# Summing |w2| on ScalarE and quantising it by expert on GpSimd, with its transposes and w1's passes in the waits of the last chain

## The reference, cut to what matters

```
def _bit_quant(W):
    scale = jnp.clip(jnp.mean(jnp.abs(W), axis=-1, keepdims=True), 1e-05, None)
    w_q = jnp.clip(jnp.round(W / scale), -1.0, 1.0) * scale
    return W + jax.lax.stop_gradient(w_q - W)
...
x = x + tanh(g_xattn) * attention(ctx, layernorm(x), ...)
x = x + tanh(g_ffn) * (silu(h @ sw1.T) @ sw2.T + gate * (silu(h @ ew1[e].T) @ ew2[e].T))
```

## Time and profile before

| | us |
|---|---|
| median of 3 runs | 617.04 (615.22 to 618.39) |
| the profiled execution | 616.48 |
| its span, first to last instruction | 614.4 |

### The profile page before, as it was taken

The page is one execution under the profiler, slowest core; times in us unless marked ns, Lnnn a source line. Parts: engine busy times, 40 slices in busy tenths (PEclk is TensorE's granted clock), DMA queues, the critical chain, the costliest instruction groups (busy, mean ns, idle before and its releaser), DMA issues.

```text
span 614.4 us, 20156 instructions
## 1 busy us (share of the span) xinstructions
PE 482.3 (79%) x6634; PEld 390.7 (64%) x6635; DVE 496.6 (81%) x1235; ACT 337.3 (55%) x943; POOL 385.8 (63%) x701
## 2 busy tenths in 40 slices
PE   0038999989989989988988998952359798899882
PEld 0015777767767766766776776641129697888882
DVE  6455998898899899899889889859976768777771
ACT  0124555665675775775675675542217566666660
POOL 5004575677887887887788788775203555555554
PEclk9999999999999999999999999995558989999997
DMA  8922122213222222222322321010121212222220
GB/s 225 247 84 81 48 63 82 68 52 90 83 63 79 81 68 71 84 72 65 96 72 62 94 76 39 15 36 19 36 56 44 72 50 66 66 69 69 59 57 13
DMA packets 74078, 44.07 MB, mean 72 GB/s; under 512 B 6866, under 2 KB 71454, under 8 KB 74032
## 3 DMA queue, kind: packets, MB, share of 16 engines
q1 hardware_dynamic: 66240, 32.39, 19.3%
q0 software_dynamic: 4352, 8.53, 4.2%
q10 hardware_dynamic: 3440, 2.55, 1.5%
HBM read 34.32 MB, written 9.65 MB: 72 GB/s over the span
## 4 chain that ended last, share of the span: by engine, by line
DVE 34%; PE 33%; issue 14%; DMA 9%; SPq 5%; POOL 2%; DVEq 1%; ACT 1%; POOLq 0%; ACTq 0%
DVE mx L528 6%; PE PS L1033 6%; DVE sc L533 5%; PE PS L1041 4%; DVE rspread L538 4%; DMA out<-lent,tin 4%; PE PS L1049 4%; PE PS L1023 3%; PE PS L1017 3%; DMA tin<-rows 3%; PE PS L1057 3%; DMA X<-in_x 2%; PE PS L1081 2%; SPq L245 2%; SPq L280 2%
## 5 line engine op out<-in xcount | busy, mean ns | idle before, releaser
L844 ACT ACTIVATE shared<-PS 124x640 f32<-124x640 f32 x128 | 89.4, 698 | 85.7 <-PE PS L1033 85.1
L528 DVE TENSOR_REDUCE mx<-PS 128x8 f32<-128x616 f32 x128 | 101.6, 794 | 17.4 <-PE PS L1023 15.4
L352 POOL TENSOR_TENSOR vm<-lent,ownhead 124x192 f32<-124x192 f32 x128 | 73.1, 591 | 60.9 <-PE PS L1049 59.8
L533 DVE TENSOR_TENSOR sc<-PS,mx 128x616 f32<-128x616 f32 x128 | 102.0, 797 | 3.2
L1033 PE MATMUL PS<-ident,sc 128*124 128x128 f32 x640 | 96.6, 282 | 3.4 <-ACT shared L844 1.5
L450 POOL DMA_INDIRECT out<-lent,tin x72 | 74.0, 1028 | 30.4 <-issue 30.4
L1033 PEld LDWEIGHTS PS<-ident,sc 128*124 128x124 f32 x640 | 70.8, 141 | 19.1 <-issue 16.8
L398 POOL DMA_INDIRECT rows<-pay,pay_i x64 | 68.4, 1068 | 12.1 <-issue 11.4
L538 DVE RECIPROCAL rspread<-PS 128x128 f32<-128x128 f32 x64 | 60.8, 950 | 16.3 <-PE PS L1049 16.3
L1041 PE MATMUL PS<-shared,ownhead 124*32 124x128 f32 x1536 | 55.2, 276 | 16.8 <-DVE X L549 16.7
L364 POOL TENSOR_TENSOR kbd_hi<-kp_hi,rowsel 128x308 fp32r<-128x308 f32 x64 | 45.3, 707 | 22.9 <-DVE kp_lo L521 21.9
(11 more groups left out here) (192 smaller groups left out, 1102.2 us busy)
## 6 DMA issues: line engine op xcount, KB each, us to landing
lent<-in_ctx SPq DMA_DIRECT2D x64, 154.0 KB
tin<-rows SPq DMA_DIRECT2D x72, 66.0 KB, 1.8
X<-in_x SPq DMA_DIRECT2D x8, 512.0 KB, 9.5
ctxq<-in_ctx SPq DMA_DIRECT2D x16, 154.0 KB
lent<-in_ctx SPq DMA_DIRECT2D x16, 128.0 KB
lent<-in_ctx SPq DMA_DIRECT2D x16, 120.0 KB
lent<-in_ctx SPq DMA_DIRECT2D x16, 94.0 KB
lent<-in_ctx SPq DMA_DIRECT2D x16, 86.0 KB
```

The lines of the kernel that those rows point to most:

```text
L352: ins = nc.gpsimd.tensor_tensor(vm[:, j % 2, v], ctxv[:, s, j, 2 * v:2 * v + CH].rearrange("r c (u v d) -> r c u v d", u=2, v=2)[:, :, :, ...
L528: nc.vector.tensor_reduce(mx[:, u], scores_of(u), AX.X, ALU.max).then_inc(mx_done, 1)
L533: nc.vector.tensor_tensor(sc[:, u, 0:2 * GK].rearrange("p (g i k) -> p g i k", g=2, k=SK), scores_of(u), mx[:, u].unsqueeze(3).broadcast_t ...
L844: nc.scalar.activation(PT[:, s, u, :], PS[0:CR, 4:6, :].rearrange("r v c -> r (v c)")[:, 0:CP * P], ACT.Exp, scale=float(1.0 / np.sqrt(HD) ...
```

## The change

|w2| is summed by ACT with nine activations (Abs with a running sum, `sum_w2`) in steps 1 and 2 of quads 1 and 2. DVE makes scales and halves from it in step 1 of quad 3. POOL quantises w2 by expert with three instructions of 128 x 256 each (`quantise_w2`): experts 0 and 1 in steps 0 and 1 of quad 14, 2 and 3 in those of quad 15, and 4 to 8 between the sorts of quad 12 and those of quad 13. The reduction of |w1| moves ahead of the step with image B + 1, its small scalings ahead of place(NQ - 2), and its last pass (the subtraction) behind top_of(NQ - 1). PE transposes w2 in three parts before and among the last chain's matmuls, and ACT copies them. DVE's reduction, four passes and nine copies for w2 are gone.

```diff
@@ gpsimd
+            def quantise_w2(e):
+                pool.wait_ge(w2_halved, 1)
+                ge(pool, w2_step, 2 * e)
+                scale = wabs2[:, e:e + 1]
+                nc.gpsimd.tensor_scalar(plus2[:], w2n[:, e], half2[:, e:e + 1], scale, ALU.is_gt, ALU.mult)
+                nc.gpsimd.tensor_scalar(minus2[:], w2n[:, e], nhalf2[:, e:e + 1], scale, ALU.is_lt, ALU.mult).then_inc(w2_step, 1)
+                pool.wait_ge(w2_step, 2 * e + 1)
+                ins = nc.gpsimd.tensor_tensor(w2n[:, e], plus2[:], minus2[:], ALU.subtract)
+                ins.then_inc(w2_step, 1)
+                if e == NE - 1:
+                    pool.wait_ge(w2_step, 2 * NE)
+                    pool.sem_inc(quantised, 1)
...
                     if j == 3 and nth >= 3:
                         sort(q - 3, 1 - s, 0)
+                    if isinstance(q, int) and q >= NQ - 2 and j < 2:
+                        quantise_w2(2 * (q - (NQ - 2)) + j)
...
             for j in range(1, QB):
                 sort(NQ - 4, 0, j)
+            for e in range(4, NE):
+                quantise_w2(e)
             for j in range(QB):
                 sort(NQ - 3, 1, j)
             root(NQ - 1, 1)
@@ vector
+                if isinstance(q, int) and q == 3 and j == 1:
+                    dve.wait_ge(w2_summed, NE)
+                    dve.wait_ge(tanh_ready, 1)
+                    step(nc.vector.tensor_scalar(wabs2[:], wabs2[:], 1.0 / F, 1e-5, ALU.mult, ALU.max))
...
             step_of(B, 0, False, True, True, 0)
+            dve.wait_ge(ffw_in, 16 * 4)
+            step(nc.vector.tensor_reduce(wabs[:], w1n[:], AX.X, ALU.add, apply_absolute_value=True))
             step_of(B + 1, 1, False, True, True, 0, logits_of=NQ - 2)
             step_of(B + 2, 2, False, False, True, 0, stats_of=NQ - 1)
             choose(NQ - 2)
-            dve.wait_ge(ffw_in, 16 * 4)
-            step(nc.vector.tensor_reduce(wabs[:], w1n[:], AX.X, ALU.add, apply_absolute_value=True))
+            step(nc.vector.tensor_scalar(wabs[:], wabs[:], 1.0 / D, 1e-5, ALU.mult, ALU.max))
...
             place(NQ - 2, 0)
             top_of(NQ - 2)
-            step(nc.vector.tensor_reduce(wabs2[:], w2n[:], AX.X, ALU.add, apply_absolute_value=True))
...
             choose(NQ - 1)
-            nc.vector.tensor_tensor(w1n[:], w1n[:], neg1, ALU.subtract).then_inc(w1_quantised, 1)
             place(NQ - 1, 1)
             top_of(NQ - 1)
+            nc.vector.tensor_tensor(w1n[:], w1n[:], neg1, ALU.subtract).then_inc(w1_quantised, 1)
             step(nc.vector.tensor_tensor(counts[:], base[:], region0[:, 0:E], ALU.subtract))
...
-            step(nc.vector.tensor_tensor(neg2, w2n[:], nhalf2[:].unsqueeze(2).broadcast_to(full), ALU.is_lt))
-            step(nc.vector.tensor_tensor(w2n[:], w2n[:], half2[:].unsqueeze(2).broadcast_to(full), ALU.is_gt))
-            step(nc.vector.tensor_tensor(w2n[:], w2n[:], neg2, ALU.subtract))
-            step(nc.vector.tensor_tensor(w2n[:], w2n[:], wabs2[:].unsqueeze(2).broadcast_to(full), ALU.mult), quantised)
-            for e in range(NE):
-                dve.wait_ge(wT_psum, e + 1)
-                nc.vector.tensor_copy(W2T[:, e], PS[:, 4 + e % 2, 0:F]).then_inc(wT_copied, 1)
@@ scalar
+            def sum_w2(experts):
+                act.wait_ge(ffw_in, 16 * 4)
+                for e in experts:
+                    nc.scalar.activation(work[:, e * F:(e + 1) * F], w2n[:, e], ACT.Abs,
+                                         accum_out=wabs2[:, e:e + 1]).then_inc(w2_summed, 1)
...
+                    if nth in (1, 2) and 0 < j < 3:
+                        sum_w2((0, 1, 2) if (nth, j) == (1, 1) else (3, 4) if (nth, j) == (1, 2) else (5, 6) if j == 1 else (7, 8))
...
+            copy_w2(range(0, 4))
             make_h(NQ - 1, range(QB))
             copy_h(NQ - 1)
+            copy_w2(range(4, 6))
             fill_pay(NQ - 2, 0)
+            copy_w2(range(6, NE))
             exp_logits(NQ - 1)
             fill_pay(NQ - 1, 1)
@@ tensor
             rank_rows(NQ - 2)
+            pe.wait_ge(quantised, 1)
...
+            transpose_w2(range(0, 4))
             transpose_h(NQ - 1, NQ)
+            transpose_w2(range(4, 6))
             pe.wait_ge(placed, NQ - 1)
             logits(NQ - 1)
+            transpose_w2(range(6, NE))
             pe.wait_ge(logits_kept, NQ)
             rank_rows(NQ - 1)
             pe.wait_ge(w1_quantised, 1)
+            pe.wait_ge(wT_copied, NE)
```

More of the change, by code:

```diff
@@ L226, in build @@
         route_step, base_ready, counts_kept, placed = (sem(x) for x in ("route_step", "base_ready", "counts_kept", "placed"))
+        w2_summed, w2_halved, w2_step = (sem(x) for x in ("w2_summed", "w2_halved", "w2_step"))
         w1_quantised, w1T_psum, w1T_copied = (sem(x) for x in ("w1_quantised", "w1T_psum", "w1T_copied"))
@@ L624, in step_of @@
                     top_of(route_of)
+                if isinstance(q, int) and q == 3 and j == 1:
+                    dve.wait_ge(w2_summed, NE)
+                    dve.wait_ge(tanh_ready, 1)
+                    step(nc.vector.tensor_scalar(wabs2[:], wabs2[:], 1.0 / F, 1e-5, ALU.mult, ALU.max))
+                    step(nc.vector.tensor_scalar(half2[:], wabs2[:], 0.5, None, ALU.mult))
+                    step(nc.vector.tensor_scalar(nhalf2[:], wabs2[:], -0.5, None, ALU.mult))
+                    step(nc.vector.tensor_scalar(wabs2[:], wabs2[:], tgf[:], None, ALU.mult), w2_halved)
                 if j == 2 and stats_of is not None:
@@ L652, in _ @@
             choose(NQ - 2)
[L654 to L655 removed]
+            step(nc.vector.tensor_scalar(wabs[:], wabs[:], 1.0 / D, 1e-5, ALU.mult, ALU.max))
+            step(nc.vector.tensor_scalar(half[:], wabs[:], 0.5, None, ALU.mult))
+            step(nc.vector.tensor_scalar(nhalf[:], wabs[:], -0.5, None, ALU.mult))
             place(NQ - 2, 0)
             top_of(NQ - 2)
[L658 to L664 removed]
             full = [P, NE, FB, D]
@@ L927, in _, with copy_w2 @@
             exp_logits(NQ - 2)
+            def copy_w2(experts):
+                for e in experts:
+                    act.wait_ge(wT_psum, e + 1)
+                    nc.scalar.copy(W2T[:, e], PS[:, e % 4, 0:F]).then_inc(wT_copied, 1)
+            copy_w2(range(0, 4))
             make_h(NQ - 1, range(QB))
             copy_h(NQ - 1)
+            copy_w2(range(4, 6))
             fill_pay(NQ - 2, 0)
+            copy_w2(range(6, NE))
             exp_logits(NQ - 1)
@@ L1133, in _, with transpose_w2 @@
             rank_rows(NQ - 2)
+            pe.wait_ge(quantised, 1)
+            def transpose_w2(experts):
+                for e in experts:
+                    if e >= 4:
+                        pe.wait_ge(wT_copied, e - 3)
+                    for f in range(FB):
+                        ins = nc.tensor.transpose(PS[:, e % 4, f * P:(f + 1) * P], w2n[:, e, f * P:(f + 1) * P], ident[:])
+                    ins.then_inc(wT_psum, 1)
+            transpose_w2(range(0, 4))
             transpose_h(NQ - 1, NQ)
+            transpose_w2(range(4, 6))
             pe.wait_ge(placed, NQ - 1)
             logits(NQ - 1)
+            transpose_w2(range(6, NE))
             pe.wait_ge(logits_kept, NQ)
@@ L1146, in _ @@
                 ins.then_inc(w1T_psum, 1)
-            pe.wait_ge(quantised, 1)
-            for e in range(NE):
-                if e >= 2:
-                    pe.wait_ge(wT_copied, e - 1)
-                for f in range(FB):
-                    ins = nc.tensor.transpose(PS[:, 4 + e % 2, f * P:(f + 1) * P], w2n[:, e, f * P:(f + 1) * P], ident[:])
-                ins.then_inc(wT_psum, 1)
             def load_experts(first_tile, n):
```

10 lines of the change are left out of this document (2 added, 8 removed).

## The result

The changed kernel takes 640.32 us in the median of 4 runs (639.34 to 640.68), the kernel before 616.38 (4 runs): 1.0376 times as long, 95% interval 1.0345 to 1.0407. That is slower, as forecast, but by 24 us instead of 10, and above the range. The page of the changed kernel: its span, the busy time of each engine, the chain that ended last by engine, and one group (line, engine, shape, count, busy us, mean ns, idle time ahead of it and its releaser).

A forecast was written before the change was run, and what follows sets the result against it. The tables' end, reached through the root in POOL's queue, was taken to bound the start of the experts' stage. Last chain 7.6, quads 14 and 15 1.7, quads 1 to 3 0.8, less 0.5: 9.6 us on 616.48, 626.0 us; range 618.5 to 633.

The forecast's parts named there:

- SyncE's queue: From tables to first split: pads and tile loads cover DVE's w2 work, so removing it gains only 0.5 us.
- the reserve of 4.9 us: Last chain: PE has the last logits 4.9 us before DVE takes them, so the root's chain may slip that far.
- c: Price of one expert on POOL: 0.57 + 0.57 + 0.72 + 0.1 = 1.95 us, between 1.6 and 3.3.
- the blocking: Last chain: DVE's two large w1 passes hold POOL's sorts ahead of the root of quad 15, 3.1 us.
- The loop: Experts 0 to 3 in quads 14 and 15 make POOL late: +1.7 us, 0.5 to 4 by an expert's price.
- Quads 1 to 3: ACT's sums (0.3 us) and DVE's four small operations (0.5) delay the loop: +0.8 us, 0 to 2.5.
- The w1 reduction: Last chain: moved ahead of the residual, it delays that and every later step of the chain by 2.0 us.
- (b): Rival: POOL's comparisons are dear, an expert costs 2.8 us, time 631 us; chance 0.13.
- (a): Rival: the sorts are not held by DVE's passes, 3.1 us less, time 623.0 us; chance 0.10.
- (d): Rival: POOL lets the root go on time, an expert costing 0.9 us; faster, 615 us; chance 0.06.
- (c): Rival: the reserve takes most of POOL's lateness, expert at 1.5 us, no blocking; no measurable change, 618.9 us; chance 0.09.
- The rule: Skill's inference that DVE's tensor_tensor leaves descriptor generation free, so sorts run at 0.96 us, time 623.0; forecast followed the trace instead.

The follow-up runs named there:

- experiments 1 to 3: changed kernel without the five experts ahead of quad 13's sorts, 628.76 us; without the four in quads 14 and 15, 630.61; without any, 614.41.
- experiment 6: kernel before with only the reduction of |w1| moved ahead of the step with image B + 1: 618.71 us, ratio 1.0042.
- Experiment 1: changed kernel without the five experts that POOL quantises ahead of quad 13's sorts: 628.76 us.
- experiments 10 and 7: kernel before without DVE's four w2 passes, ratio 0.9994; kernel before with ACT summing |w2| and copying transposes, w2's scales made behind the tables, ratio 0.9968.
- experiment 9: changed kernel with the five experts behind the root of quad 15 and w2's transposes and copies behind those of w1: 629.75 us.

## Why the prediction was wrong

**What held.** SyncE's queue, not DVE, sets the time from the tables to the first split: 17.9 us in the changed kernel and 17.9 to 18.0 in experiments 1 to 3, and taking the passes away gave 0.52 us in one profile, 0.1 in another, and nothing that 12 runs can tell. The root behind the experts, in POOL's queue, sets the tables; the reserve of 4.9 us is used up first; behind the last logits the path costs 12.75 us (455.35 to 468.10) where I had 13.1 and before 12.2. The sign, and the place, were right: what failed is the size of two terms.

**The step that failed is the price of an expert on POOL.** I wrote c = 1.95 and bounded it by 3.3; it is 3.44, above even the ceiling: two comparisons of 1.22 (just under the ceiling of 1.24 each), 0.73 for the subtraction (0.72 forecast) and 0.27 of gaps between them where I had 0.1. The nearest row was an affine_select of 0.40 us at 128 columns, and I took 0.57 for 256. It was another instruction with another price, and I had written myself that no tensor_scalar was in the trace. I kept the ceiling of 1.24 a comparison for c but let the range run only from c = 1.5, below my own floor of 1.6, to 3.0.

By the same steps: five experts in the last chain cost 16.9 us instead of 9.75, and 20.65 with the blocking. The blocking was forecast on the sorts, 3.1 us; it fell on the last expert's comparisons, which took 3.33 and 2.85 us beside passes at 433.67 to 439.32 us, 3.7 us in all. Its size was nearly right, by luck: I had drawn it on other instructions, and where POOL meets the passes depends on c.

**The loop.** I had 1.7 us for quads 14 and 15, and 0.5 to 4 as its bounds. The experts cost 8.2 there, twice the upper bound, and c alone does not explain that, for the bound was to hold at c = 3.3. My own steps give more: two experts of 3.2 us, less 1.61 of idle and 1.0 of reserve, are 3.8 us a quad and 7.6 for both. I had counted quad 14 at half a microsecond; it took 5.3. So the second step that failed is the slack I let the loop absorb, above all in quad 14. Quads 1 to 3 cost 2.0 instead of 0.8. ScalarE's sums cost nothing (0.3 forecast): DVE's maxima are 0.56 us late in quad 0, where no sum has run yet, and 0.57 at image 13, behind all of them. At image 14 they are 2.61 late: the four small operations between cost 2.0 instead of 0.5, and that step of 2.0 is in all five profiles of kernels that have them and in none of the other profiles of the table. The remaining 1.8 of the 12.1 us is no part of the change that I can name: 0.55 is there from quad 0 on, and 1.2 gathers between quads 4 and 13, where the other profiles, with the same code there, fall behind that of before by 0.3 to 2.2. The timeline of DVE there in the changed kernel:

```profile
122.69 0.63 DVE L650 TENSOR_SCALAR half<-wabs 128x9 f32<-128x9 f32 x1
123.35 0.63 DVE L651 TENSOR_SCALAR nhalf<-wabs 128x9 f32<-128x9 f32 x1
124.02 0.23 DVE L652 TENSOR_SCALAR wabs<-wabs,tgf 128x9 f32<-128x9 f32 x1
```

The second and third of the four took 0.63 us, the last 0.23: each ends 0.03 us behind one of POOL's two products for the keys (122.58 to 123.29 and 123.24 to 123.95 us), so they look held by it, as the DVE passes hold POOL.

**The w1 reduction.** 2.0 us forecast; 3.4 in experiment 6, the rest with TensorE's clock, which fell in other profiles without it. In the changed kernel this was hidden behind POOL's queue and cost nothing. Experiment 1 laid it bare: of the 15.5 us by which its root was late, 10.8 were there at image 63, and the other 4.7 lie in the stretch of the reduction and the fallen clock. That stands behind POOL's queue as a second lateness almost as long, which experiment 1's expectation left out.

**The sum again with the measured terms:** 12.1 (loop) + 20.9 (root against the loop) - 4.8 (reserve) + 0.55 (behind the logits) - 0.6 (split) = 28.15 us, as the two splits show. Of the 20.9, 20.65 are the five experts. The experts' stage took 3.9 us less in this profile. No part of the change reaches it, and it took between 152.7 and 157.5 us in the ten profiles above, with no order that follows the edits. Why it varies was not tested.

**The rivals.** (b), dear comparisons, is what happened; I gave it 0.13 and sized it at c = 2.8, which with its own terms adds up to 632 and not 631. (a) was right about the sorts: the four ahead of the root ran in 0.96 to 1.08 us each (442.14 to 447.02), held by nothing. But its 3.1 us less did not come, because two comparisons were held instead, for 3.7. (d) needed c below 0.9 and fell with its price; (c) fell with it.

**The rule.** SBUF — State Buffer in the Trainium skill (section Who interferes with whom) gives a DVE operation with two SBUF inputs as contending with a GpSimd instruction that reads SBUF. The trace agrees for instructions: 3.33 and 2.85 us instead of 1.22. For descriptor generation, which that section of the Trainium skill infers to be free of it, the changed kernel shows a sort held once more: the one at 458.92 us took 2.60 us beside the w1 subtraction at 458.16. Whether generating its descriptors or reading its row numbers from SBUF is what waits, no run here tells.

## What to carry to other kernels

Work moved to an idle engine is priced by the place in that engine's queue: look for the first instruction behind it on which the path waits, and put the new work behind that one. Before moving work off the engine that looks like the bound, subtract it on paper and ask what would be waited for next; here a queue of DMAs covered all of it, and releasing the queue earlier (with the passes cut in two beside it) gained what freeing VectorE did not. Where the trace holds no row of the very instruction, take its ceiling into the range at full width, or price it by itself first. And compare a stretch in several profiles of the same code before a microsecond or two in it is called the edit's.

## What the runs showed of the hardware that I had not expected

- GpSimd's tensor_scalar on 128 x 256 fp32 took 0.93 us with one operation and 1.21 with two, its tensor_tensor 0.61 with a broadcast operand and 0.72 with two full ones: the form with one tensor input is the dearer one.
- Behind a wait of 2.38 us TensorE's granted clock was 0.56 (1.2 GHz for most of it) where it had been 1.00, and the weighing took 1.51 us instead of 0.86 (experiment 6). A wait of 0.47 us at the same place left the clock at 1.00 in four profiles of the same code and was followed by 0.66 and 0.67 in two others (experiments 10 and 7): 2.65 us for the stretch or 3.75, with nothing in the code between them.
- The blocking goes both ways, and small operations are held as well: an operation on four columns and a copy took 2.5 us on GpSimd beside a VectorE pass (experiment 9), a VectorE operation on 9 columns 0.63 us beside a GpSimd product, and a VectorE pass of 2.56 us took 2.82 beside GpSimd's comparisons.
